# Layer 1's lanes in 22 short steps a unit, and the four products with v of a half issued as one block

## The reference

```python
qkv = x @ Wqkv_w.T + Wqkv_b                    # 16 heads of 16
scores = einsum('bthd,bshd->bhts', q, k) / 4   # causal mask, softmax
ctx = einsum('bhts,bshd->bthd', attn, v)
q2 = conv1d(ctx, conv_w, padding=1) + conv_b   # 3 taps along the rows
ctx2 = _causal_attn(q2, k, v)                  # the same k and v again
out = ctx2 @ out_w.T + out_b
```

## Time and profile before

| | us |
|---|---|
| median of 3 runs | 2157.86 |
| lowest, highest | 2154.74, 2158.21 |
| profiled execution | 2160.07 |
| its span | 2158.2 |
| TensorE busy | 1836.4 |
| VectorE busy | 1255.3 |
| ScalarE busy | 1020.4 |
| GpSimd busy | 363.6 |

### The profile page before, as it was taken

How to read it: one execution, slowest core, us unless ns; L and a number is a source line. 1 busy time by engine, 2 the same in 40 slices (tenths; PEclk the granted TensorE clock), 3 DMA queues, 4 the chain that set the end, 5 groups by cost and what they waited for, 6 DMA issues and landing times.

```text
span 2158.2 us, 31797 instructions
## 1 busy us (share of the span) xinstructions
PE 1836.4 (85%) x10767; PEld 901.2 (42%) x10777; DVE 1255.3 (58%) x3777; ACT 1020.4 (47%) x2048; POOL 363.6 (17%) x555
## 2 busy tenths in 40 slices
PE   3475799999989999995489797998998898889987
PEld 2341344554534454541234343444444444444433
DVE  4554455655555444552554676767676767776663
ACT  0242456555545555564244244544454445445444
POOL 2215221121101111112443101001010100000000
PEclk8557899999999999998599899999999999999999
DMA  7245343434364444423104235555453545554350
GB/s 144 70 141 143 67 80 72 84 72 79 67 171 94 69 62 69 62 33 85 38 22 65 31 53 60 75 70 75 63 74 54 73 67 68 77 68 59 50 60 21
DMA packets 145969, 155.87 MB, mean 72 GB/s; under 512 B 26009, under 2 KB 132785, under 8 KB 145809
## 3 DMA queue, kind: packets, MB, share of 16 engines
q1 hardware_dynamic: 123872, 114.75, 34.0%
q0 software_dynamic: 10048, 14.44, 3.7%
q10 hardware_dynamic: 11888, 24.64, 3.6%
HBM read 55.95 MB, written 33.72 MB: 42 GB/s over the span
## 4 chain that ended last, share of the span: by engine, by line
PE 65%; DVE 15%; ACT 6%; issue 5%; DMA 4%; POOL 4%; SPq 2%; DVEq 0%; ACTq 0%; POOLq 0%
PE p_PV L843 12%; PE p_S L826 9%; PE p_S L804 9%; DVE p_S L1195 6%; PE p_Ma L1019 4%; PE p_Mb L898 4%; PE p_S L921 4%; ACT t_R L1629 3%; PE p_Ma L765 3%; SPq L1986 2%; PE p_Ma L773 2%; PE p_Mb L765 2%; PE p_S L830 2%; POOL idd L1878 1%; PE p_Mb L921 1%
## 5 line engine op out<-in xcount | busy, mean ns | idle before, releaser
L1629 ACT ACTIVATE t_R<-p_S 128x512 f32<-128x512 f32 (+1 forms) x1216 | 670.8, 577 | 503.7 <-PE p_S L830 347.0
L1195 DVE CUSTOM_DVE_ANT_0 p_S<-p_S,t_NM 128x128 f32<-128x128 f32 (+3 forms) x1024 | 472.3, 522 | 90.2 <-PE p_S L804 86.7
L804 PE MATMUL p_S<-t_R 96*128 96x512 bf16 (+3 forms) x1536 | 456.0, 340 | 64.2 <-DVE t_mx L1195 32.2
L1201 DVE TENSOR_REDUCE t_mx<-p_S 128x1 f32<-128x512 f32 x512 | 346.6, 686 | 260.1 <-PE p_S L804 247.0
L826 PE MATMUL p_S<-t_R 99*128 99x512 bf16 (+3 forms) x1536 | 468.4, 332 | 21.9 <-ACT t_R L1629 8.7
L843 PE MATMUL p_PV<-t_R 128*17 128x512 f32 (+3 forms) x3072 | 325.2, 495 | 12.4 <-ACT t_R L1629 10.0
L804 PEld LDWEIGHTS p_S<-t_R 96*128 96x128 bf16 x1536 | 135.8, 99 | 395.2 <-issue 136.5
L826 PEld LDWEIGHTS p_S<-t_R 99*128 99x128 bf16 x1536 | 150.0, 98 | 175.5 <-issue 79.6
L1844 POOL CAST t_spl<-t_rr 128x512 bf16<-128x512 f32 x80 | 49.0, 612 | 969.9 <-DVE t_rr L1153 969.8
L830 PE MATMUL p_S<-t_NM 128*128 128x128 bf16 x1024 | 196.1, 220 | 0.0
L1195 DVE DVE_READ_ACCUMULATOR2_ANT t_mx<- 128x1 f32 x1024 | 145.0, 142 | 0.0
(11 more groups left out here) (245 smaller groups left out, 2124.1 us busy)
## 6 DMA issues: line engine op xcount, KB each, us to landing
t_R<-t_spl SPq DMA_DIRECT2D x480, 128.0 KB
t_R<-in_w ACTq DMA_DIRECT2D x32, 512.0 KB, 7.6
t_R<-ks SPq DMA_DIRECT2D x96, 128.0 KB
ks<-t_spl SPq DMA_DIRECT2D x16, 384.0 KB, 7.3
hTd<-t_NM SPq DMA_DIRECT2D x39, 128.0 KB
ysd<-t_NM SPq DMA_DIRECT2D x39, 128.0 KB
t_NM<-hTd SPq DMA_DIRECT2D x39, 128.0 KB, 2.3
ysd<-t_NM POOLq DMA_DIRECT2D x39, 128.0 KB, 3.1
```

The source lines that it names most:

```text
L804: t = self.nc.tensor.matmul(bank[:, z, :], qa[0:96, h, qb * 128:(qb + 1) * 128], ka[0:96, h, 0:n], start=True, stop=True)
L1195: x = nc.vector.tensor_tensor_reduce(out=sc, in0=sc, in1=m.maskq[:, 512 - n:512], scale=1.0, scalar=NEG, op0=ALU.add, op1=ALU.max, accum_o ...
L1201: nc.vector.tensor_reduce(m.mx[:, g, i:i + 1], m.S1[s1_bank(k)][:, :], AX.X, ALU.max).then_inc(s.s1_read, 1)
L1629: nc.scalar.activation(m.P1X[kb][j0 // per] if u.causal else m.P[p % 2][:, j0:j0 + per, :], m.s2_bank(k)[:, 0:per * n].rearrange("p (j n) ...
```

## The change

`pipeline`, `LATE` and `LATE2` go. `layer1` now interleaves all four lanes one step each:

```diff
-    pipeline(UNITS1, 0, e.expp, e.maxp, e.pre1, lambda i, lane: [(lane(e.fin1, i - 1), 3)])
+    def lane(f, i):
+        return f(UNITS1[i]) if 0 <= i < len(UNITS1) else none()
+    for i in range(len(UNITS1) + 1):
+        interleave([(lane(e.expp, i), 1), (lane(e.maxp, i + 1), 1), (lane(e.pre1, i + 2), 1), (lane(e.fin1, i - 1), 1)])
```

The lanes of all engines are written once, in the common class, and call small methods that each engine fills in. The lane of exponentials has 11 steps a half. A half's four products come together, in the second step of the next half, and what closes the half follows step by step:

```diff
+    def exponentials(self, u):
+        for g in range(2):
+            for kb in range(4):
+                n0 = 128 * kb
+                per = (1, 1, 2, 4)[kb]
+                for j0 in range(0, 4, per):
+                    self.scores(u, g, kb, j0, per, n0)
+                    self.products()
+                    yield
+            self.due.append([2, u, g])
...
+    def products(self):
+        for d in self.due:
+            d[0] -= 1
+        while self.due and self.due[0][0] == 0:
+            _, u, g = self.due.pop(0)
+            for kb in range(4):
+                self.product(u, g, kb)
+            self.closing = self.close1(u, g)
+        next(self.closing, None)
+
+    def close1(self, u, g):
+        yield
+        self.copy_o(u, g)
+        yield
+        yield
+        self.turn_o(u, g)
+        yield
+        self.divide(u, g)
+        yield
```

The lane of maxima has 11 steps a half too. What turns, splits and sends the maxima of a half runs in steps 2 and 3 of the next half, on all engines:

```diff
+    def maxima(self, u):
+        for g in range(2):
+            for qb, js in packs_of(u):
+                self.top(u, g, qb, js)
+                next(self.chain, None)
+                yield
+            self.chain = self.shift(u, g)
...
+    def shift(self, u, g):
+        yield
+        yield
+        self.turn_m(u, g)
+        self.split_m(u, g)
+        yield
+        self.rows(u, g)
+        yield
```

`pre1` issues one or two f32 matmuls a step (`fan1(u, 1)` is k's fan, `fan1(u, 0)` q's, `rest` the residue and the low parts):

```diff
+        if u.kind == 1:
+            yield from steps(3)
+            self.part(u, 0, 0)
+            yield
+            self.part(u, 0, 1)
+            yield
+            self.high1(u, 0)
+            yield
+            self.rest(u, 0)
+            self.part(u, 1, 0)
+            yield
+            self.part(u, 1, 1)
+            yield
+            self.fan1(u, 0)
+            self.high1(u, 1)
+            yield
+            self.rest(u, 1)
+            yield
+            for k in range(4):
+                self.part(u, 2, k)
+                if k == 1:
+                    self.fan1(u, 1)
+                yield
+            self.values(u)
+            return
+        soon = u.c or u.b not in (0, NB - 1)
+        yield from steps(3 if u.c else 1 if soon else 6)
+        if u.c == 0:
+            for c in range(2):
+                self.turn_c(u, c)
+                yield
+                self.keep_c(u, c)
+                yield
+        for i in range(6):
+            self.convolve(u, i)
+            if i == 3:
+                self.fan1(u, 1)
+            if soon or i % 2:
+                yield
+        self.high1(u, 0)
+        yield
+        self.rest(u, 0)
+        yield
+        self.fan1(u, 0)
+        yield
```

More of the change, by code:

```diff
@@ L138, in none @@
     return iter(())
[L141 to L147, removed]
 def steps(n):
@@ L651, in maxp, with maxp0, top, turn_m @@
     def maxp(self, u):
-        return steps(s1_uses(u) + 2 * u.causal)
+        return self.maxima(u) if u.causal else self.maxp0(u)
+    def maxp0(self, u):
+        return steps(s1_uses(u))
+    def maxima(self, u):
[5 more added lines that the diff above has]
+            self.chain = self.shift(u, g)
+        if u.n == 47:
+            yield from self.chain
+    def shift(self, u, g):
[6 more added lines that the diff above has]
+        yield
+    def top(self, u, g, qb, js): pass
+    def turn_m(self, u, g): pass
+    def split_m(self, u, g): pass
+    def rows(self, u, g): pass
     def gathers(self, b):
@@ new lines, in pre1, with part, high1, rest @@
+        yield
+        self.fan1(u, 0)
+        yield
+    def part(self, u, z, k): pass
+    def high1(self, u, z): pass
+    def rest(self, u, z): pass
+    def fan1(self, u, z): pass
+    def values(self, u): pass
+    def turn_c(self, u, c): pass
+    def keep_c(self, u, c): pass
+    def convolve(self, u, i): pass
+    def fin1(self, u):
+        if u.kind != 2 or u.c != 1:
+            return
+        yield from steps(6)
+        for c in range(2):
+            self.turn_f(u, c)
+            yield
+            self.keep_f(u, c)
+            yield
+        yield from steps(4)
+        for h in range(2):
+            self.out(u, h)
+            yield
+            self.add_out(u, h)
+            yield
+        self.store(u)
@@ L678, in expp, with turn_f, keep_f, out @@
+    def turn_f(self, u, c): pass
+    def keep_f(self, u, c): pass
+    def out(self, u, h): pass
+    def add_out(self, u, h): pass
+    def store(self, u): pass
     def expp(self, u):
+        if u.causal:
+            yield from self.exponentials(u)
+            return
         for g in range(2):
             for kb in range(4):
[L682 to L686, removed]
+                for j0 in range(4):
+                    self.scores(u, g, kb, j0, 1, 0)
+                    if self.late is not None and j0 >= 1:
@@ L1173, in value, with maxp0 @@
             ALU.add).then_inc(s.v_done, 1)
[L1175 to L1183, removed]
+    def maxp0(self, u):
         nc, e, m, s = self.nc, self.e, self.m, self.s
         for g in range(2):
-            for qb, js in packs_of(u):
-                n = 128 * (qb + 1) if u.causal else 512
+            for qb, (j,) in packs_of(u):
```

466 lines of the change are left out of this document (235 added, 231 removed).

## The result

The changed kernel takes 2218.34 us, median of 4 runs (2214.24 to 2219.86), the kernel before 2158.03 in runs beside it: ratio 1.0272, with its 95% interval 1.0243 to 1.0301. It is 60 us slower, where 11 were forecast, and outside the range. The profiled execution's span is 2212.4 us. VectorE's and ScalarE's busy time are as before, within 12 us; TensorE's is 1844.8 for 1836.4. The mean granted clock over the span is 0.907, before it was 0.935.

What follows compares the result with a forecast made beforehand. Neither TensorE nor VectorE was full; the change would make rows behind fans on the SP queue bind. Terms without clock summed to -4.3 us, clock +15.6, so +11.3: forecast 2169 us, own range 2158 to 2182, widened to 2105 to 2186.

Steps and rivals of the forecast that it cites:

- The queue argument: SP queue in layer 1: row DMAs issued behind 12 fans and `ks` land 16.3 us after the first fan's issue.
- C: Layer 1 iteration whose `pre1` projects q, k, v; forecast at 28.5 us against 27.6 before.
- Rival 1: Layer 1 rounds: fans don't bind, a round is 104.2 us, total 2076; chance 0.27 wholly or in part.
- Rival 2: Layer 1 rounds: fans bind but the clock holds, total 2154 us; chance 0.18.
- the clock term: TensorE's clock falls after stalls of about 4 us at 13 iteration starts, 1.2 us each: +15.6 us.
- A and B: Layer 1 iterations whose `pre1` convolves, the first also carrying `fin1`; forecast 33.0 us against 32.71 and 25.9 against 27.51.
- Rival 3: Layer 1 starts: clock low through each whole stall and the block, 2.8 us at 13 starts, total 2190; chance 0.10.
- The rounds' +0.5: Net change of one four-iteration round of layer 1 without the clock: +0.5 us, +3 in six rounds.
- The block: Four products of a half issued together: TensorE 2.53 us instead of 3.01 apart, 0.48 us saved per half.
- VectorE's hole: VectorE gets no maxima during the block of products and idles about 1.1 us per half.
- The late convolutions for batch 0 and 7: Both wait for K's fan, the first 5.91 us; sending K's fan before Q's saves only 1.5 us each.
- The order of starting: SP queue: descriptors start in order, so rows wait behind the fans rather than overtaking them; the forecast sum rests on this.

## Why the prediction was wrong, by its own steps

**The queue argument held.** C was forecast at 28.5 us and is 28.55 in the round shown, where its clock is nearly whole (0.96; the other five take 29.3 to 31.0 at 0.89 to 0.94); the residue starts 9.03 us after the start (forecast 9.5), the first fan 11.71 (12.2), and the rows land 16.8 after it (16.3). The round without the clock's loss was forecast at 115.9 and is 115.45. Rival 1, fans that don't bind, was priced at 104.2 a round and 2076 us; with small fans it is 103.41 and 2073.7. Rival 2, fans bind and the clock holds, was priced at 2154 and is 2155.7. These two experiments make the rivals' conditions true one at a time, and the prices stood.

**The step that failed is the clock term.** "Stalls of about 4 us at 13 iteration starts", "I take 1.2", "13 x 1.2 = 15.6": with the measured 62.7 in its place, -4.3 + 62.7 = +58.4, and 2216 us for the measured 2218. It was undersized in both factors.

- The price. I had bounds of 0 and 3.3 us for a long stall, and took 1.2 from a row of a stall of 2.06 us. The row after 5.91 us, at 0.50, was the nearer one to a stall that leaves TensorE with nothing; by the filled long stalls alone a start costs 2.8.
- The count. The same layout had A and B end on landing rows too, at 33.0 and 25.9 us, which means a wait at the starts of B and C. I added up their lengths and did not count them as stalls, although showed 0.66 after 2.06 us. They stall 1.4 to 2.5 us, 14 times, and filling them alone gave 32.0 us, 2.3 each. Rival 3, with 2.8 for 13 starts, had the price right and missed the count, and so stopped at 2190.

**Smaller steps.** The rounds' +0.5 in the sum is 115.9 less 115.51, so 0.4 and 2.3 in six for the 3 that I took; it changes nothing. The block holds TensorE 2.29 us, from 1562.68 to 1564.97 (forecast 2.53, apart 3.01). VectorE's hole behind it was taken as 1.1 us; in C's two halves it is 1.77 and 2.13, the idle times ahead of the first two rows of VectorE's timeline below (the third is q's residue, 9.03 us after C's start). A half without f32 work, B's second with small fans, takes 10.56 (forecast 10.3). The late convolutions for batch 0 and 7 were to lose 1.5 us of their stall; they wait 6.59 and 6.73 for 5.91. These and the other ends are some microseconds each, and with the clock filled their sum is right within 2 us, so errors among them cancelled.

```profile
1591.53 0.43 DVE L1387 CUSTOM_DVE_ANT_0 p_S<-p_S,t_NM 128x256 f32<-128x256 f32 x1 [1.77 <-PE p_S L978]
...
1604.62 0.43 DVE L1387 CUSTOM_DVE_ANT_0 p_S<-p_S,t_NM 128x256 f32<-128x256 f32 x1 [2.13 <-PE p_S L978]
...
1596.97 0.75 DVE L1345 SCALAR_TENSOR_TENSOR t_rr<-p_Ma,t_BQK,t_spl 128x512 f32<-128x512 f32 x1
```

**The order of starting was half the story.** The prediction read the landings as an order of starting in one queue, by the Trainium skill, "DMA: Bandwidth & Descriptors", Two DMAs through the same engine are not ordered. On SyncE's queue the sum by it came out right. But rows on ScalarE's queue landed no sooner beside the fans, 7.1 to 7.6 us, so here a second queue did not help: from 1602 to 1608 us SyncE's queue moved 747 packets and ScalarE's none. The Trainium skill, "DMA: Bandwidth & Descriptors", Queues, rings and completion order, says that each DMA engine takes turns between the queues it has work for, a packet at a time. By that the rows on a queue of their own should have passed between the fans' packets; with 747 to none the trace does not bear it out here. Whether the rows' packets stood ready at the engines all this time, or were held before them, no run shows.

**The block.** I priced it by 0.48 us of TensorE's time a half, a gain, and by a hole of 1.1 us in VectorE's. That the products also release q's fan, as shown above, had no term; in the changed kernel, whose q fan leaves 11.7 us after the start, it could not bind. Spread, the kernel is 18 us faster at the late rows and 50 to 68 slower where the fan is early.

## What to carry to other kernels

When a layout shows that every stage of a pipeline ends on a transfer, count a stall at every stage, the short ones too, and price each with what the clock loses behind it: here the waits at 28 starts cost 63 us beyond their own length, nearly all of the 67 that the new order gains where the fans are small. A transfer that must be early is helped by issuing the large ones sooner, not by another queue; and an order that takes slack out of one engine should first be tried with the transfers made small, which shows at once what it is worth (67 us faster here) and what they cost it (145).

## What the runs showed of the hardware

- Of 14 waits of TensorE of 1.4 to 2.5 us, 12 were followed by a granted clock of 0.50 for part of the time behind them, as 0.63 over the 3.15 us from 1681.85; behind the ones of 1.41 us at 1561.81 and 1.62 at 1587.94 it stayed at 1.00. They cost 2.3 us each in the mean. The 14 waits of 3.6 to 5.2 us were followed by 0.50, as over the 3.51 us from 1616.49, and cost 2.8 each.
- 200 bf16 matmuls of 512 columns in 600 us, issued into these waits, kept the clock at 1.00 and gave 62.7 us over the whole kernel. A version with 205 of them, where most of the waits were gone, was 40 us slower than the same with 36.
- Three DMAs of 4 KB on a queue of their own took 7.1 to 7.6 us beside 12 of 128 KB on another queue, 1.7 alone; in the 6 us after their issue the other queue moved 747 packets and theirs none.
